# Folds, row maxima and biases of two score tiles at once in the sums pass of a fake-quantised attention

## The chip, the cores and the metric

The kernel runs on one core of a Trainium2 chip. Time is device time in microseconds (us) of one execution of the whole program; lower is better. Engines are named as in the profile: PE (TensorE), DVE (VectorE), ACT (ScalarE), POOL (GpSimd) and SP (SyncE, which issues transfers).

## The reference

The program is a small vision tower: an embedding of 8 images to 8 x 256 tokens of width 192, a first attention with 12 heads whose tensors are all quantised to 8 bits, a mixture of 8 experts, a second attention and a second mixture. Only the first attention is touched. Cut to what matters:

```python
def fake_quant(x):                       # one scale for the whole tensor
    scale = max(|x|) / 127
    return clip(round(x / scale), -127, 127) * scale
scores = einsum('bhqd,bhkd->bhqk', q, k) / sqrt(16)
scores = fake_quant(scores)              # 8 images x 12 heads x 256 x 256
attn = fake_quant(softmax(scores, -1))   # needs the largest weight of all rows
ctx = einsum('bhqk,bhkd->bhqd', attn, v)
```

The quantisation of `attn` needs the greatest softmax weight of the whole tensor before the first weight can be rounded. So the kernel goes over all scores once for the sums of the exponentials (the sums pass), then once more for the weights.

## The kernel before, in words

The program is written engine by engine; each engine runs its own instruction list in order, and semaphores (`wait_ge`, `then_inc`) tie them together. The first attention consists of blocks that follow one another:

- A block takes the greatest score of all 24 tiles (L1022) and, from it, the columns `f_s` and `ns_s`, which hold the scale of the scores.
- The **sums pass** (the block of L1048 to L1145) goes over the same 24 tiles. A tile `n` is four heads of one image: 128 partitions by 8 rows of 256 scores, 2048 values to a partition. PE computes its scores into one half of `pp`, which has two (L922, for the first three images L912); it may overwrite a half when the tile two before has been read. DVE quantises the tile (L1098, from `pp` into `v16t`, which the profile calls `m_pieces`), takes the maximum of its left and right halves into `fold` (L1106), folds 128 to 64 in place (L1114), takes each row's maximum (L1102, `vmax`) and multiplies it to a bias (L1110, `nb`, in the profile `a_nb`). ACT then takes the exponential of each of the eight rows with that bias and adds it up (L1084, eight instructions to a tile, each with an accumulator read).
- DVE's list is interleaved by hand: the steps of tile `n` stand between those of tile `n - 1`, so that a step never follows directly on the one whose result it needs. `v16t`, `vmax` and `nb` have room for all 24 tiles, so DVE never waits for ACT there.
- Behind the tiles, a serial end: reciprocals of the sums of tiles 0 to 22 (L1126) once ACT has finished tile 22, those of the last tile (L1129), a maximum (L1130), an all-reduce on POOL (L1073), a logarithm on ACT (L1089), a split into three parts on DVE (L1137 to L1141), transposes on PE (L1057) and copies (L1144). Then the block of the weights begins (L1183 and on).

ACT's wait before tile `n` is `act.wait_ge(biased, n + 1)`, where `biased` counts the instructions of L1110. The short letters used further down: Q is the quantise step, F the first fold, f the second fold, R the row maxima, B the bias, each with its tile's number.

Of the kernel before, what the change touches and what calls it, by code (L numbers as in the profile page):

```python
# [9 lines left out]
F16 = mybir.dt.float16  # L10
# [3 lines left out]
ALU = mybir.AluOpType  # L14
ACT = mybir.ActivationFunctionType
AX = mybir.AxisListType
# [3 lines left out]
S, D = 256, 192  # L20
T = B * S
P = 128
# [13 lines left out]
HALF = 1536.0  # L36
# [790 lines left out]
def attention0(c, a, scratch, out, proj, pieces, held):  # L827
# [5 lines left out]
    sc, top, peak, room, wout, col = proj.sc, proj.top, proj.peak, proj.room, proj.wout, proj.col  # L833
    with ExitStack() as s:
# [21 lines left out]
        with ExitStack() as s1:  # L856
# [38 lines left out]
            with ExitStack() as s2:  # L895
                TILES = B * H // 4
                mxs = c.sb("a0_mxs", [P, TILES], F32, s2)
                ex = c.sb("a0_ex", [P, 2, 8, S], BF16, s2)
                fold = c.sb("a0_fold", [P, 2, 8, P], F16, s2)
                pp = c.ps("a0_pp", [P, 2, 4, 2 * S], F32, s2)  # L900

                def score(pe, n, k, padded=None):
# [16 lines left out]
                    for j in range(4):  # L919
                        h = 4 * g + j  # L920
                        for qt in range(2):
# [5 lines left out]
                scored, read, chain, peaked, reduced, xrounded, lifted, padded, rounded, stored = (  # L927
                    c.sem(f"a0m_{n}") for n in ("scored", "read", "chain", "peaked", "reduced", "xrounded", "lifted",
                                                "padded", "rounded", "stored"))
                scored_again = c.sem("a0s_scored")  # L930
# [110 lines left out]
                v16t = v16.rearrange("p b (g k) t q -> p (b g) (k t) q", k=4)  # L1041
                vmaxt = vmax[:].rearrange("p b (g k) t -> p (b g) (k t)", k=4)
                nbt = nb[:].rearrange("p b (g k) t -> p (b g) (k t)", k=4)
                sumst = sums[:].rearrange("p b (g k) t -> p (b g) (k t)", k=4)
                c.retire()
                with nc.Block(no_gpsimd_drain=True) as block:

                    @block.tensor  # L1048
                    def _(pe):
                        for n in range(2, TILES):  # L1050
                            pe.wait_ge(read, n - 1)
                            score(pe, n, B + n // 3).then_inc(scored_again, 1)
                        for n in range(2):
                            pe.wait_ge(split, n + 1)
                            for k in range(8):
                                t = 8 * n + k
                                last = nc.tensor.transpose(  # L1057
                                    pr[n][:, k, :], parts[:, t // 2, t % 2].rearrange("p r h -> p (r h)"),
                                    c.identb[:])
                            last.then_inc(turned, 1)  # L1060

                    @block.sync
                    def _(sp):
                        sp.dma_start(sel, a["sel6"]).then_inc(loaded, 16)
                        for img in range(PADDED + 2, B):
                            sp.wait_ge(scored_again, 3 * (img - 1))
                            load_heads(sp, LOADED + img - PADDED)
                        sp.wait_ge(loaded, 16)

                    @block.gpsimd  # L1070
                    def _(pool):
                        pool.wait_ge(peaked, 1)
                        pool.partition_all_reduce(peak[:, 6:7], top[:, 6:7], P, RMAX).then_inc(reduced, 1)  # L1073

                    @block.scalar
                    def _(act):
                        scale = act.alloc_register("a0_scale")
                        act.reg_load(scale, col["s_s"][0:1, :].bitcast(I32))
                        for n in range(TILES):
                            act.wait_ge(biased, n + 1)  # L1080
                            if n >= 2:
                                act.wait_ge(summed, n - 1)
                            for r in range(8):
                                last = act.activation(ex[:, n % 2, r], v16t[:, n, r, :], ACT.Exp,  # L1084
                                                      bias=nbt[:, n, r:r + 1], scale=scale,
                                                      accum_out=sumst[:, n, r:r + 1])
                            last.then_inc(summed, 1)
                        act.wait_ge(scaled, 1)
                        act.activation(flat_lg, rc[:, 0:COUNT], ACT.Ln, scale=col["i_a"]).then_inc(logged, 1)  # L1089

                    @block.vector
                    def _(dve):
                        v = nc.vector
                        link = Chain(dve, chain).link
                        for n in range(TILES + 1):
                            if n < TILES:
                                dve.wait_ge(scored_again, n + 1)
                                v.tensor_scalar(v16t[:, n], pp[:, n % 2].rearrange("p j (t q) -> p (j t) q", q=S),  # L1098
                                                col["f_s"], HALF, ALU.mult, ALU.add).then_inc(read, 1)
                            if n >= 1:  # L1100
                                dve.wait_ge(folded, 2 * n)
                                v.tensor_reduce(vmaxt[:, n - 1], fold[:, (n - 1) % 2, :, 0:P // 2], AX.X, ALU.max)\  # L1102
                                 .then_inc(maxed, 1)
                            if n < TILES:
                                dve.wait_ge(read, n + 1)
                                v.tensor_tensor(fold[:, n % 2], v16t[:, n, :, 0:P], v16t[:, n, :, P:S], ALU.max)\  # L1106
                                 .then_inc(folded, 1)
                            if n >= 1:
                                dve.wait_ge(maxed, n)
                                v.tensor_scalar(nbt[:, n - 1], vmaxt[:, n - 1], col["ns_s"], None, ALU.mult)\  # L1110
                                 .then_inc(biased, 1)
                            if n < TILES:
                                dve.wait_ge(folded, 2 * n + 1)
                                v.tensor_tensor(fold[:, n % 2, :, 0:P // 2], fold[:, n % 2, :, 0:P // 2],  # L1114
                                                fold[:, n % 2, :, P // 2:P], ALU.max).then_inc(folded, 1)
                        dve.wait_ge(biased, TILES)

                        def part(r, n):
                            return parts[:, 4 * n:4 * n + 4, :, r, :].rearrange("p b t h -> p b h t")

                        v.memset(parts[:, :, :, 0, :], -HALF)
                        v.memset(parts[:, :, :, 5, :], 0.0)
                        for n in range(2):
                            v.tensor_scalar(part(1, n), vmax[:, 4 * n:4 * n + 4], -1.0, HALF, ALU.mult, ALU.add)
                        dve.wait_ge(summed, TILES - 1)
                        link(v.reciprocal(rc[:, 0:COUNT - LAST], flat_sums[:, 0:COUNT - LAST]))  # L1126
                        link(v.tensor_reduce(rc[:, COUNT:COUNT + 1], rc[:, 0:COUNT - LAST], AX.X, ALU.max))
                        dve.wait_ge(summed, TILES)
                        link(v.reciprocal(rc[:, COUNT - LAST:COUNT], flat_sums[:, COUNT - LAST:COUNT]))  # L1129
                        v.tensor_reduce(top[:, 6:7], rc[:, COUNT - LAST:COUNT + 1], AX.X, ALU.max).then_inc(peaked, 1)  # L1130
                        dve.wait_ge(reduced, 1)
                        scale_of(link, v, peak[:, 6:7], col["s_a"])
                        v.reciprocal(col["i_a"], col["s_a"]).then_inc(scaled, 1)
                        dve.wait_ge(logged, 1)
                        for n in range(2):
                            rest = lg[:, 4 * n:4 * n + 4]
                            link(v.tensor_scalar(rest, rest, col["i_s"], None, ALU.mult))  # L1137
                            for r in range(2, 4):
                                link(v.tensor_copy(part(r, n), rest))
                                link(v.tensor_tensor(rest, rest, part(r, n), ALU.subtract))  # L1140
                            v.tensor_copy(part(4, n), rest).then_inc(split, 1)  # L1141
                        for n in range(2):
                            dve.wait_ge(turned, n + 1)
                            v.tensor_copy(rows.rearrange("r b (t q) -> r (b t) q", t=2)[:, 8 * n:8 * n + 8, :],  # L1144
                                          pr[n]).then_inc(kept, 1)  # L1145
# [2252 lines left out]
```

## Time and profile before

| | us |
|---|---|
| time, three runs | 1001.4, 1001.75, 1006.43 (median 1001.75) |
| span of the profiled execution, first to last instruction | 1014.8 |
| PE, DVE, ACT, POOL busy in the span | 743.6, 697.2, 672.0, 345.9 |
| first to last exponential of the sums pass (starts) | 170.9 to 264.8 |
| first to last quantise step of the sums pass (starts) | 163.7 to 253.4 |

The three times were taken without the profiler; of the profiled execution only the span is known, and it is 13.05 us (1.3%) longer than the median. Times inside the trace count from the first instruction. A row of the timeline begins with the start and the duration; a duration on DVE or ACT overlaps with the start of the next instruction, so what an instruction costs its engine is read from one start to the next.

### The profile page before, as it was taken

How to read it: one execution, taken by the hardware profiler on the slowest of the kernel's cores; microseconds unless marked ns; L12 is line 12 of the kernel's file. 1: busy time of each engine (PE TensorE's matmuls, PEld its weight loads, DVE VectorE, ACT ScalarE, POOL GpSimd, SP SyncE). 2: the span in 40 equal slices, each digit the busy share in tenths (PEclk: the TensorE clock that was granted, in tenths of full speed). 3: DMA queues.
4: the chain of work that ended last, by engine and by line, in shares of the span. 5: the costliest groups of instructions: out<-in, count | busy, mean ns of one | idle time of the engine just before them, and what ended most of it. 6: DMA issues, size and time to landing. Idle time of an engine off the chain costs nothing. (4 is left out here: it accounts for less than half of the span.)

```text
span 1014.8 us, 19178 instructions
## 1 busy us (share of the span) xinstructions
PE 743.6 (73%) x7062; PEld 537.8 (53%) x7063; DVE 697.2 (69%) x1403; ACT 672.0 (66%) x1229; POOL 345.9 (34%) x260
## 2 busy tenths in 40 slices
PE   2987373344299547999997488867775898999985
PEld 1464141122277324589996444324444467899974
DVE  4159998999599888745443475986998875444542
ACT  1267956999799657755554369578983661676663
POOL 6620460000000000357776424580001202477763
PEclk9979555555599768999999879555556798999999
DMA  5224485000121318623333456380003942233332
GB/s 168 71 90 130 138 234 169 1 23 1 47 75 69 122 45 289 200 54 59 57 56 47 90 233 254 117 297 35 2 2 105 344 169 71 37 54 58 59 45 32
DMA packets 61883, 105.26 MB, mean 104 GB/s; under 512 B 9678, under 2 KB 43618, under 8 KB 61554
## 3 DMA queue, kind: packets, MB, share of 16 engines
q1 hardware_dynamic: 45426, 87.77, 25.6%
q0 software_dynamic: 16384, 16.53, 10.4%
q8 instruction: 45, 0.74, 0.3%
q14 instruction: 28, 0.23, 0.1%
HBM read 76.39 MB, written 27.87 MB: 103 GB/s over the span
## 5 line engine op out<-in xcount | busy, mean ns | idle before, releaser
L2301 DVE COPY m_xgT<-m_px 128x768 f16<-128x768 f16 (+1 forms) x46 | 22.9, 497 | 123.5 <-PE m_px L2146 123.5
L2268 ACT ACTIVATE m_pu<-m_pu,m_b,m_unit 128x256 f32<-128x256 f32 (+1 forms) x138 | 63.5, 509 | 60.9 <-PE m_pu L2178 58.4
L2309 DVE SCALAR_TENSOR_TENSOR m_hT<-m_pu,m_unit,m_hT 128x512 f16<-128x512 f32 (+1 forms) x138 | 86.4, 663 | 17.4 <-ACT m_hT L2261 17.2
L1084 ACT ACTIVATE a_ex<-m_pieces,a_nb 128x256 bf16<-128x256 f16 x192 | 94.6, 560 | 5.4 <-DVE a_nb L1110 5.4
L922 PE MATMUL a_pp<-a_room 16*128 16x256 bf16 x240 | 56.1, 412 | 39.8 <-DVE m_pieces L1098 31.9
L2272 ACT ACTIVATE m_pu<-m_pu,m_unit 128x512 f32<-128x512 f32 (+1 forms) x69 | 41.1, 597 | 62.7 <-PE m_pu L2178 61.7
L2261 ACT ACTIVATE m_hT<-m_pu,m_unit 128x512 f16<-128x512 f32 (+1 forms) x138 | 81.6, 636 | 0.0
L2112 POOL DMA_INDIRECT m_xg<-xn_d,m_token x70 | 70.0, 1000 | 32.1 <-issue 20.6
L2120 POOL DMA_INDIRECT out_h<-m_yo,m_token x39 | 62.1, 1593 | 40.6 <-DVE m_yo L2319 28.8
L2120 POOL DMA_INDIRECT h_d<-m_yo,m_token x39 | 62.1, 1592 | 37.3 <-DVE m_yo L2319 18.0
L2178 PE MATMUL m_pu<-m_xgT,m_w 128*128 128x256 f16 (+1 forms) x690 | 70.4, 261 | 1.3 <-DVE m_xgT L2301 1.3
L2178 PE MATMUL m_pu<-m_xgT,m_pieces 128*128 128x256 f16 (+1 forms) x690 | 67.9, 256 | 1.7 <-issue 1.0
L922 PEld LDWEIGHTS a_pp<-a_room 16*128 16x128 bf16 x240 | 30.3, 136 | 65.6 <-DVE m_pieces L1098 39.0
L2178 PEld LDWEIGHTS m_pu<-m_xgT,m_w 128*128 x690 | 59.7, 100 | 8.8 <-DVE m_xgT L2301 1.7
L2197 PE MATMUL m_py<-m_pieces,m_hT 128*128 x702 | 61.6, 246 | 2.9 <-issue 1.4
L2197 PE MATMUL m_py<-m_w,m_hT 128*128 x702 | 63.0, 246 | 0.0
L2178 PEld LDWEIGHTS m_pu<-m_xgT,m_pieces 128*128 x690 | 58.5, 98 | 8.0 <-issue 1.8
L2197 PEld LDWEIGHTS m_py<-m_pieces,m_hT 128*128 128x128 f16 x702 | 57.4, 98 | 4.3 <-issue 2.6
L2197 PEld LDWEIGHTS m_py<-m_w,m_hT 128*128 128x128 f16 x702 | 58.5, 98 | 0.0
L1098 DVE TENSOR_SCALAR m_pieces<-a_pp,a_sc 128x2048 f16<-128x2048 f32 x24 | 56.4, 2351 | 1.4 <-PEq L931 1.4
L2545 POOL TENSOR_TENSOR hv_parts<-hv_raw,hv_parts 128x1536 f16<-128x1536 f32 (+1 forms) x16 | 43.8, 2739 | 39.3 <-ACT hv_raw L2540 30.3
L1022 DVE TENSOR_REDUCE a_mxs<-a_pp 128x1 f32<-128x2048 f32 x24 | 53.0, 2284 | 1.9 <-PE a_pp L922 1.3
(488 smaller groups left out, 1914.2 us busy)
## 6 DMA issues: line engine op xcount, KB each, us to landing
m_pieces<-in_m_w SPq DMA_DIRECT2D x11, 768.0 KB, 5.1
a_early_w<-in_m_w SPq DMA_DIRECT2D x10, 768.0 KB
hv_raw<-in_m_w SPq DMA_DIRECT2D x8, 768.0 KB, 6.2
w1h_d<-hv_parts SPq DMA_DIRECT2D x8, 768.0 KB, 4.1
m_w<-w1h_d SPq DMA_DIRECT2D x8, 768.0 KB, 9.0
m_pieces<-in_m_w SPq DMA_DIRECT2D x8, 576.0 KB, 5.3
a_room<-in_m_w SPq DMA_DIRECT2D x8, 576.0 KB, 3.6
hv_raw<-in_m_w SPq DMA_DIRECT2D x8, 576.0 KB, 5.9
```

Source lines behind the costliest of these rows:

```text
L922: last = nc.tensor.matmul(pp[:, n % 2, j, qt * S:(qt + 1) * S], qkb[:, load % 2, h, qt * P:(qt + 1) * P], qkb[:, load % 2, H + h, :], star ...
L1022: v.tensor_reduce(mxs[:, n:n + 1], pp[:, n % 2], AX.XY, ALU.max, apply_absolute_value=True).then_inc(read, 1)
L1084: last = act.activation(ex[:, n % 2, r], v16t[:, n, r, :], ACT.Exp, bias=nbt[:, n, r:r + 1], scale=scale, accum_out=sumst[:, n, r:r + 1])
L1098: v.tensor_scalar(v16t[:, n], pp[:, n % 2].rearrange("p j (t q) -> p (j t) q", q=S), col["f_s"], HALF, ALU.mult, ALU.add).then_inc(read, 1)
L2112: pool.indirect_dma_start(xg[:, m % 2, j, :], None, xn_d, bass.IndirectOffsetOnAxis(ap=token[:, n:n + 1], axis=0)).then_inc(got[m % 2], 16)
L2120: pool.indirect_dma_start(total_d, bass.IndirectOffsetOnAxis(ap=token[:, n:n + 1], axis=0), yo[:, m % 2, j, :], None, compute_op=ALU.add). ...
L2178: last = nc.tensor.matmul(pu[:, u, q // 2, (q % 2) * w:(q % 2 + 1) * w], w1_bytes[:, bass.ds(e * (2 * W) + up_place(wpart, tail, q), 2 * P ...
L2197: last = nc.tensor.matmul(py[:, j * D:(j + 1) * D], hT[:, u, hpart, q * w + j * P:q * w + (j + 1) * P], w2_bytes[:, bass.ds(e * (2 * FC * ...
L2261: act.activation(hT[:, u, 0, n * 2 * w:(n + 1) * 2 * w], pu[:, u, n, 0:2 * w], ACT.Identity, scale=unit[:, 1:2]).then_inc(hhigh, 1)
L2268: act.activation(pu[:, u, n, q * w:(q + 1) * w], pu[:, u, n, q * w:(q + 1) * w], ACT.Relu, bias=b1[:, bass.ds(e * FC + 2 * n + q, 1)], sca ...
L2309: last = v.scalar_tensor_tensor(hT[:, u, 1, third], pu[:, u, n, 0:2 * w], unit[:, 1:2], hT[:, u, 0, third], ALU.mult, ALU.subtract)
L2545: self.c.nc.gpsimd.tensor_tensor(parts[:, 1, :], raw, parts[:, 0, :], ALU.subtract).then_inc(self.lowered, 1)
```

## The change

In the sums pass the tiles are put into 14 groups: tiles 0 and 1 alone, ten pairs (2, 3) to (20, 21), tiles 22 and 23 alone. F, f, R and B are done once for a group, so for a pair with twice the width; Q stays one instruction per tile. The second fold gets a tensor of its own, `fold2`, instead of folding in place. ACT's wait before tile `n` becomes a wait for the bias of its group.

```diff
--- before.py
+++ after.py
@@ -897,6 +897,10 @@
                 mxs = c.sb("a0_mxs", [P, TILES], F32, s2)
                 ex = c.sb("a0_ex", [P, 2, 8, S], BF16, s2)
                 fold = c.sb("a0_fold", [P, 2, 8, P], F16, s2)
+                fold2 = c.sb("a0_fold2", [P, 2, 8, P // 2], F16, s2)
+                GROUPS = [(0, 1), (1, 2)] + [(n, n + 2) for n in range(2, TILES - 2, 2)] + \
+                         [(TILES - 2, TILES - 1), (TILES - 1, TILES)]
+                group_of = [g for g, (n0, n1) in enumerate(GROUPS) for _ in range(n0, n1)]
                 pp = c.ps("a0_pp", [P, 2, 4, 2 * S], F32, s2)
 
                 def score(pe, n, k, padded=None):
@@ -1077,7 +1081,7 @@
                         scale = act.alloc_register("a0_scale")
                         act.reg_load(scale, col["s_s"][0:1, :].bitcast(I32))
                         for n in range(TILES):
-                            act.wait_ge(biased, n + 1)
+                            act.wait_ge(biased, group_of[n] + 1)
                             if n >= 2:
                                 act.wait_ge(summed, n - 1)
                             for r in range(8):
@@ -1092,28 +1096,36 @@
                     def _(dve):
                         v = nc.vector
                         link = Chain(dve, chain).link
-                        for n in range(TILES + 1):
-                            if n < TILES:
-                                dve.wait_ge(scored_again, n + 1)
-                                v.tensor_scalar(v16t[:, n], pp[:, n % 2].rearrange("p j (t q) -> p (j t) q", q=S),
-                                                col["f_s"], HALF, ALU.mult, ALU.add).then_inc(read, 1)
-                            if n >= 1:
-                                dve.wait_ge(folded, 2 * n)
-                                v.tensor_reduce(vmaxt[:, n - 1], fold[:, (n - 1) % 2, :, 0:P // 2], AX.X, ALU.max)\
+                        def quantize(n):
+                            dve.wait_ge(scored_again, n + 1)
+                            v.tensor_scalar(v16t[:, n], pp[:, n % 2].rearrange("p j (t q) -> p (j t) q", q=S),
+                                            col["f_s"], HALF, ALU.mult, ALU.add).then_inc(read, 1)
+
+                        for g in range(len(GROUPS) + 1):
+                            n0, n1 = GROUPS[g] if g < len(GROUPS) else (TILES, TILES)
+                            if g >= 1:
+                                p0, p1 = GROUPS[g - 1]
+                                fold_1, fold_2 = fold[:, 0:p1 - p0], fold2[:, 0:p1 - p0]
+                            if n0 < n1:
+                                quantize(n0)
+                            if g >= 1:
+                                dve.wait_ge(folded, 2 * g - 1)
+                                v.tensor_tensor(fold_2, fold_1[:, :, :, 0:P // 2], fold_1[:, :, :, P // 2:P], ALU.max).then_inc(folded, 1)
+                            if n0 + 1 < n1:
+                                quantize(n0 + 1)
+                            if g >= 1:
+                                dve.wait_ge(folded, 2 * g)
+                                v.tensor_reduce(vmaxt[:, p0:p1], fold_2, AX.X, ALU.max)\
                                  .then_inc(maxed, 1)
-                            if n < TILES:
-                                dve.wait_ge(read, n + 1)
-                                v.tensor_tensor(fold[:, n % 2], v16t[:, n, :, 0:P], v16t[:, n, :, P:S], ALU.max)\
-                                 .then_inc(folded, 1)
-                            if n >= 1:
-                                dve.wait_ge(maxed, n)
-                                v.tensor_scalar(nbt[:, n - 1], vmaxt[:, n - 1], col["ns_s"], None, ALU.mult)\
+                            if n0 < n1:
+                                dve.wait_ge(read, n1)
+                                v.tensor_tensor(fold[:, 0:n1 - n0], v16t[:, n0:n1, :, 0:P],
+                                                v16t[:, n0:n1, :, P:S], ALU.max).then_inc(folded, 1)
+                            if g >= 1:
+                                dve.wait_ge(maxed, g)
+                                v.tensor_scalar(nbt[:, p0:p1], vmaxt[:, p0:p1], col["ns_s"], None, ALU.mult)\
                                  .then_inc(biased, 1)
-                            if n < TILES:
-                                dve.wait_ge(folded, 2 * n + 1)
-                                v.tensor_tensor(fold[:, n % 2, :, 0:P // 2], fold[:, n % 2, :, 0:P // 2],
-                                                fold[:, n % 2, :, P // 2:P], ALU.max).then_inc(folded, 1)
-                        dve.wait_ge(biased, TILES)
+                        dve.wait_ge(biased, len(GROUPS))
 
                         def part(r, n):
                             return parts[:, 4 * n:4 * n + 4, :, r, :].rearrange("p b t h -> p b h t")
```

Both lists of DVE begin with the steps of tile 0 and the quantise step of tile 1 (before: Q0, F0, f0, Q1, R0, F1, B0, f1; changed: Q0, F0, Q1, f0, R0, F1, B0). Then, in the kernel before, from the quantise step of tile 2 on; `m_pieces` is the quantised tile, which Q writes and F reads, and the last word of a row is the size of the output:

```order
L1098 TENSOR_SCALAR m_pieces<-a_pp,a_sc 128x2048
L1102 TENSOR_REDUCE a_vmax<-a_fold 128x8
L1106 TENSOR_TENSOR a_fold<-m_pieces 128x1024
L1110 TENSOR_SCALAR a_nb<-a_vmax,a_sc 128x8
L1114 TENSOR_TENSOR a_fold<-a_fold 128x8x64
L1098 TENSOR_SCALAR m_pieces<-a_pp,a_sc 128x2048
L1102 TENSOR_REDUCE a_vmax<-a_fold 128x8
L1106 TENSOR_TENSOR a_fold<-m_pieces 128x1024
L1110 TENSOR_SCALAR a_nb<-a_vmax,a_sc 128x8
L1114 TENSOR_TENSOR a_fold<-a_fold 128x8x64
```

The same stretch of DVE's list in the changed kernel, from the quantise step of tile 2 to the bias of the pair 2, 3:

```order
L1101 TENSOR_SCALAR m_pieces<-a_pp,a_sc 128x2048
L1113 TENSOR_TENSOR a_fold<-a_fold 128x512
L1101 TENSOR_SCALAR m_pieces<-a_pp,a_sc 128x2048
L1118 TENSOR_REDUCE a_vmax<-a_fold 128x8
L1122 TENSOR_TENSOR a_fold<-m_pieces 128x2048
L1126 TENSOR_SCALAR a_nb<-a_vmax,a_sc 128x8
L1101 TENSOR_SCALAR m_pieces<-a_pp,a_sc 128x2048
L1113 TENSOR_TENSOR a_fold<-a_fold 128x1024
L1101 TENSOR_SCALAR m_pieces<-a_pp,a_sc 128x2048
L1118 TENSOR_REDUCE a_vmax<-a_fold 128x16
L1122 TENSOR_TENSOR a_fold<-m_pieces 128x2048
L1126 TENSOR_SCALAR a_nb<-a_vmax,a_sc 128x16
```

Before, the bias of tile 1 (the first L1110 shown) stands behind the quantise step of tile 2 alone. Now it (the first L1126) stands behind those of tiles 2 and 3 and behind the fold of the pair 2, 3, which has 2048 outputs. The bias of tile 2 (before the second L1110 shown, now the L1126 with 128x16) stands behind the quantise steps of tiles up to 3 before and up to 5 now.

The last steps of DVE's list in the changed kernel, from the last pair on:

```order
L1101 TENSOR_SCALAR m_pieces<-a_pp,a_sc 128x2048
L1113 TENSOR_TENSOR a_fold<-a_fold 128x1024
L1118 TENSOR_REDUCE a_vmax<-a_fold 128x16
L1122 TENSOR_TENSOR a_fold<-m_pieces 128x1024
L1126 TENSOR_SCALAR a_nb<-a_vmax,a_sc 128x16
L1101 TENSOR_SCALAR m_pieces<-a_pp,a_sc 128x2048
L1113 TENSOR_TENSOR a_fold<-a_fold 128x512
L1118 TENSOR_REDUCE a_vmax<-a_fold 128x8
L1122 TENSOR_TENSOR a_fold<-m_pieces 128x1024
L1126 TENSOR_SCALAR a_nb<-a_vmax,a_sc 128x8
L1113 TENSOR_TENSOR a_fold<-a_fold 128x512
L1118 TENSOR_REDUCE a_vmax<-a_fold 128x8
```

The bias of the pair 20, 21 (the first row with 128x16 of L1126 here) stands behind one quantise step of tile 22; tiles 22 and 23 follow singly.

## Rows read from the trace of the kernel before

**Rows 1.** Busy time and granted clock, 90 us of the sums pass.

```profile
core 0: us, PE busy (x) PEld busy (x) DVE busy (x) ACT busy (x) POOL busy (x), PEclk, DMA share, GB/s
171.00:261.00 90.00, 31.30 (x160) 15.68 (x160) 88.12 (x117) 90.00 (x367) 0.00 (x0) 0.50 0.03 7
```

**Rows 2.** Instructions by line and shape: busy, mean ns, idle before, releaser.

```profile
L1084 ACT ACTIVATE a_ex<-m_pieces,a_nb 128x256 bf16<-128x256 f16 x192 | 94.6, 560 | 5.4 <-DVE a_nb L1110 5.4
L1098 DVE TENSOR_SCALAR m_pieces<-a_pp,a_sc 128x2048 f16<-128x2048 f32 x24 | 56.4, 2351 | 1.4 <-PEq L931 1.4
L1106 DVE TENSOR_TENSOR a_fold<-m_pieces 128x1024 f16<-128x1024 f16 x24 | 16.5, 689 | 0.0
```

**Rows 3.** Timeline of ACT, start of the sums pass: start, duration.

```profile
170.86 0.51 ACT L1084 ACTIVATE a_ex<-m_pieces,a_nb 128x256 bf16<-128x256 f16 x1 [5.43 <-DVE a_nb L1110]
...
174.32 0.50 ACT L1084 ACTIVATE a_ex<-m_pieces,a_nb 128x256 bf16<-128x256 f16 x1
174.82 0.50 ACT L1084 ACTIVATE a_ex<-m_pieces,a_nb 128x256 bf16<-128x256 f16 x1
```

**Rows 4.** Timeline of DVE, start of the sums pass.

```profile
163.70 2.35 DVE L1098 TENSOR_SCALAR m_pieces<-a_pp,a_sc 128x2048 f16<-128x2048 f32 x1 [1.38 <-PEq L931]
166.08 0.69 DVE L1106 TENSOR_TENSOR a_fold<-m_pieces 128x1024 f16<-128x1024 f16 x1
166.81 0.43 DVE L1114 TENSOR_TENSOR a_fold<-a_fold 128x512 f16<-128x512 f16 x1
167.15 2.34 DVE L1098 TENSOR_SCALAR m_pieces<-a_pp,a_sc 128x2048 f16<-128x2048 f32 x1
169.41 0.68 DVE L1102 TENSOR_REDUCE a_vmax<-a_fold 128x8 f32<-128x512 f16 x1
170.00 0.68 DVE L1106 TENSOR_TENSOR a_fold<-m_pieces 128x1024 f16<-128x1024 f16 x1
170.60 0.22 DVE L1110 TENSOR_SCALAR a_nb<-a_vmax,a_sc 128x8 f32<-128x8 f32 x1
170.74 0.42 DVE L1114 TENSOR_TENSOR a_fold<-a_fold 128x512 f16<-128x512 f16 x1
171.07 2.35 DVE L1098 TENSOR_SCALAR m_pieces<-a_pp,a_sc 128x2048 f16<-128x2048 f32 x1
...
174.52 0.23 DVE L1110 TENSOR_SCALAR a_nb<-a_vmax,a_sc 128x8 f32<-128x8 f32 x1
```

**Rows 5.** Timeline of PE, the scores of a late tile.

```profile
208.77 1.88 PE L922 MATMUL a_pp<-a_room 16*128 16x256 bf16 x8 [2.04 <-DVE m_pieces L1098]
```

**Rows 6.** Timeline of DVE, last tiles and what follows.

```profile
256.87 0.23 DVE L1110 TENSOR_SCALAR a_nb<-a_vmax,a_sc 128x8 f32<-128x8 f32 x1
257.01 0.43 DVE L1114 TENSOR_TENSOR a_fold<-a_fold 128x512 f16<-128x512 f16 x1
257.47 0.69 DVE L1102 TENSOR_REDUCE a_vmax<-a_fold 128x8 f32<-128x512 f16 x1
258.19 0.23 DVE L1110 TENSOR_SCALAR a_nb<-a_vmax,a_sc 128x8 f32<-128x8 f32 x1
...
261.63 1.30 DVE L1126 RECIPROCAL a_early_w<-a_sums 128x184 f32<-128x184 f32 x1 [2.33 <-ACT a_ex L1084]
```

**Rows 7.** Timeline, the end of ACT and the hand-over.

```profile
264.82 0.63 ACT L1084 ACTIVATE a_ex<-m_pieces,a_nb 128x256 bf16<-128x256 f16 x1
265.22 0.32 ACT L1084 ACTIVATION_READ_ACCUMULATOR a_ex<-m_pieces,a_nb 128x1 f32 x1
...
265.65 0.20 DVE L1129 RECIPROCAL a_early_w<-a_sums 128x8 f32<-128x8 f32 x1 [2.33 <-ACT a_ex L1084]
...
273.62 0.58 PE L1183 MATMUL a_pt<-a_early_w 72*128 72x512 bf16 x1 [1.13 <-PEq L1046]
```

**Rows 8.** Shapes near the widened instructions, by line.

```profile
L3053 DVE TENSOR_REDUCE a_neg<-a_pa 128x4 f32<-128x1024 f32 x24 | 29.2, 1219 | 0.0
...
L1943 DVE TENSOR_TENSOR m_tvals<-m_tvals,m_gate 128x624 f16<-128x624 f16 x8 | 6.1, 805 | 0.0
```

## The prediction

> **What bounds the kernel now.** I read the busy time of the engines over the sums pass first, because the change touches nothing else. In 90 us of it ACT is busy for all 90.00 us and DVE for 88.12; PE is busy for a third, and the granted clock is 0.50, the lower of its two levels (1.2 GHz) [rows 1]. So two engines look full, and a table of busy time can't tell which of them sets the end. The list by line tells more: the 192 exponentials of L1084 have 5.4 us of idle time before them in all, in a single wait, for the first bias; DVE's steps L1098 and L1106 have 1.4 and 0.0 [rows 2]. After its first instruction ACT never waits.
>
> The two paces come from starts in the timeline. ACT: the first exponential starts at 170.86, the first of tile 1 at 174.82 [rows 3], the 192nd at 264.82 [rows 7]; 93.96 us over 191 steps is 0.492 us each, 3.935 us a tile. DVE: the bias of tile 0 starts at 170.60 and that of tile 1 at 174.52 [rows 4], 3.92 us a tile. They differ by 0.4%, and ACT is the slower. The bias of tile 1 is ready at 174.52 + 0.23 = 174.75, and ACT takes it at 174.82: DVE delivers just in time at the start, and from there gets ahead by 0.01 us a tile. The last bias is ready at 258.42, the last tile but one starts on ACT about at 257.4, so all of the last tile's 3.9 us run while DVE has no tile work. What ends the pass is ACT: DVE's reciprocals start at 261.63 and 265.65, right behind tiles 22 and 23 [rows 6, 7], and the next block's first matmul at 273.62 follows in series. In the whole stretch the core moves 7 GB/s [rows 1], so no transfer hides a delay. A microsecond more or less at the end of ACT's exponentials is one in the kernel's time.
>
> **The change, part by part.** What DVE's steps cost is read from start to start in [rows 4]: Q 2.26 (167.15 to 169.41), R 0.595 (169.41 to 170.00), F 0.60 (170.00 to 170.60), f 0.335 (170.74 to 171.07), B 0.14 (170.60 to 170.74), the last because f then waits for F. Sum 3.92.
>
> *Removed:* 40 of the 96 narrow steps (14 each of F, f, R, B in place of 24). *Widened:* ten of each. No row shows an f16 maximum of 2048 outputs. From 512 to 1024 outputs a fold goes from 0.335 to 0.60, so 0.52 ns an output and about 0.065 fixed; the fold of a pair is then 0.065 + 2048 x 0.52 = 1.13, its second fold 0.60. R of 1024 inputs: a reduction of that size elsewhere takes 1.219 us where the one of 512 here takes 0.68 [rows 4, 8], 0.54 more, so 1.13. Bounds: simply twice the narrow step (1.20, 0.67, 1.19) on one side, and no fixed part at all, 1.06, 0.53, 1.06, on the other. B I take as 0.10, between 0.07 (half of what it costs now, since f no longer follows at its heels) and 0.14. A pair costs DVE 2 x 2.26 + 0.60 + 1.13 + 1.13 + 0.10 = 7.48 us, against 7.84 before: 0.36 us less. ACT needs 7.87 for it, so in the steady state this saving is worth nothing.
>
> *Moved:* the price is at the start, where there is no lead. Tile 0 hardly changes: f0 goes behind Q1, the dependent pair F0, f0 (0.73 apart, 166.08 to 166.81) is split, so Q1 starts at 166.68, f0 at 168.94, R0 0.46 later (the distance of 257.01 to 257.47 [rows 6]) at 169.40, and B0 at 170.59 as before. ACT starts at 170.86.
>
> Then B1 stands behind Q2, f1, Q3, R1 and the fold of the pair: 170.59 + 0.10 + 2.26 + 0.335 + 2.26 + 0.595 + 1.13 = 177.27. From a bias to ACT it is 0.26 (170.60 to 170.86), so tile 1 starts at 177.53 in place of 174.82: **a stall of 2.71 us**.
>
> B(2,3) stands behind Q4, f(2,3), Q5, R(2,3) and the fold of 4, 5: 177.27 + 0.10 + 2.26 + 0.60 + 2.26 + 1.13 + 1.13 = 184.75. Tile 2 starts at 185.01; ACT ended tile 1 at 177.53 + 3.935 = 181.46: **a second stall of 3.55 us**.
>
> B(4,5) comes 7.48 later, ready for ACT at 192.49; ACT ends tile 3 at 185.01 + 7.87 = 192.88. No third stall, by 0.39 us, and each further pair adds 0.39 to the lead. From here ACT runs 22 tiles through: it ends at 185.01 + 22 x 3.935 = 271.6, before 170.86 + 94.4 = 265.3. The sum is 2.71 + 3.55 = **6.3 us later**. With the bounds of B and of the wide steps: all at the low ends 6.3 - 0.07 x 3 (two wide folds and R) - 0.07 (f) - 0.03 x 2, about 6.0; all at the high ends 6.3 + 0.27 + 0.08 = 6.6, and a pair then costs 7.72, still under 7.87.
>
> What else could wait: PE writes a tile's scores in 1.88 us [rows 5], at the earliest after Q of the tile two before. Between the end of Q2 and the start of Q4 DVE spends f, Q3, R, F and B, about 5.2 us, so PE stays hidden; the loads of further heads, issued by the number of scored tiles, have as many tiles' time as before. At the end DVE delivers B22 and B23 alone and finishes earlier than now, but ACT then lags by more. Instructions of PE, SP, POOL and ACT are the same in number and order.
>
> *A rule and the rows.* DVE's fixed part of 0.065 us a step is what the change saves, 0.36 us a pair. The Trainium skill, "VectorE: DVE Perf Modes", section "The TRN2 errata — SBUF-src ops pay a fixed extra latency per instruction", says that latency is exposed between instructions and that tiles of at least 512 elements spread it out; that speaks for the change. By the rule alone the pass would end earlier with DVE, by about 3.4 us (below); by the rows, which put the end on ACT, it ends 6.3 later. This case's trace agrees that there is such a fixed part.
>
> **The rivals.**
>
> *A. Two stalls, as worked out: +6.3 us.*
>
> *B. DVE sets the pace in a run without the profiler (not slower, or less so).* The profiled span is 1.3% longer than the median, and ACT's lead over DVE as the limit is only 0.4%. Let a tile cost ACT t. Before, the end is the latest of 170.86 + 24t, 257.13 + 2t and 258.45 + t (biases of tiles 22 and 23 [rows 6]). After, B(18,19) is ready at 184.75 + 8 x 7.48 + 0.26 = 244.85, B(20,21) 0.10 + 2.26 + 0.60 + 1.13 + 0.60 and some waiting later, about at 249.7, B23 two narrow groups on, at 255.0; the end is the latest of 185.01 + 22t, 244.85 + 6t, 249.7 + 4t and 255.0 + t. At t = 3.86 the difference is +5.1, at 3.6 +2.1, and it turns at t = 3.07, from 257.13 + 2t = 244.85 + 6t; at 2.5 it is -2.3, and -3.4 is the most that it could ever give. So even a coarser grain of DVE's deliveries takes back what its shorter list gains, unless ACT is a fifth faster than the rows say. Against: the exponentials are 0.49 us apart while DVE works and still when it has stopped (264.82 less 170.86 above spans both), and there is no sign that recording slows them. For: I can't see the pace outside the profile, and 2% less on ACT already brings the loss to 5 us. The point from which it decides is a tile of 3.07 us.
>
> By the same page of the Trainium skill, "VectorE: DVE Perf Modes", same section, an exponential of 256 elements costs ScalarE 224 + 256 cycles at 1.2 GHz, an estimate of 0.40 us; this trace has 0.40 from its start to the start of the accumulator read (264.82 to 265.22 [rows 7]) and 0.09 more for the read. Were the read free outside the profile, the page's figure would make t 3.2 and the change +0.5 us; no run here shows that.
>
> *C. Wide steps cost more than in proportion.* If the f16 maximum lost its rate on this shape, at the price of the nearest slower row, 0.805 us for 624 outputs [rows 8], some 1.04 ns an output, a pair's F would be 2.2 and f 1.13, a pair 9.08 us, above ACT's 7.87. ACT would wait at each pair: B(18,19) at 178.3 + 9 x 9.1 = 260.2, then 5.2 to B(20,21) and four tiles on ACT: 281.4, +16 us. The decision point is 1.54 us for F. Against: the strides of the rows are those of the narrow step, only the count doubles.
>
> *D. The delay is partly given back later.* The block behind starts in series and its engines then wait for each other as before; nothing is in flight that the 6 us could hide. But 750 us of program follow, with clocks that vary, so a few microseconds either way are possible: +2 to +5.
>
> *E. The later program falls better into place and the whole gets over 5 us faster.* No row speaks for it.
>
> **How the numbers follow.** A 0.70, B 0.10, C 0.04, D 0.12, E 0.04. The sum was made against the profiled span: 1014.8 + 6.3 = 1021.1. I carry the same 6.3 to the median of the timed runs, since it consists of waits for DVE steps of fixed length: 1001.75 + 6.3 = 1008.05, **1008.0 us**, 0.63% slower. Half a per cent, 5.0 us, is about what a measurement of this kernel can tell from no change. A's own range is +5 to +7.5; with B and D in it the range goes from 1003.5 to 1010.5, which holds A but for a few hundredths, and most of B and D. Slower by over 0.5%: A but for 0.06 below 5 us, and C: 0.68. Within 0.5%: that 0.06, B and D: 0.28. Faster: E, 0.04.
>
> **What would show it.** In the profile of the changed kernel: ACT's exponentials with two more waits for the bias, 2.7 us before tile 1 and 3.5 us before tile 2, and none after; the folds with 2048 outputs at 1.2 us each by duration; DVE's last bias near 254.7 in place of 258.19, more idle time on DVE before the first reciprocal; the first matmul of the next block at 279.9. A third wait of ACT would mean that a pair costs DVE over 7.87. The prediction is wrong if ACT's pace between the stalls isn't 3.935, or if the time differs from the profile's difference by more than a microsecond or two.

## The result

The changed kernel takes 1008.2 us (median of six runs), the kernel before 1000.8 us in the six runs beside it. The ratio is 1.0069, with a 95% interval of 1.0044 to 1.0094: 4.4 to 9.4 us slower.

The page of the changed kernel begins so:

```profile
span 1007.0 us, 19138 instructions
...
PE 732.1 (73%) x7062; PEld 533.6 (53%) x7063; DVE 695.0 (69%) x1363; ACT 671.4 (67%) x1229; POOL 346.0 (34%) x260
```

Read alone, this misleads: the profiled execution of the slower kernel is 7.8 us shorter than the one shown of before. A span holds the whole program, and what happened outside the pass differed between these two executions by more than the change is worth (the last experiment comes back to it). So everything below is read inside the pass, from the start of the first quantise step to the first matmul of the block behind (L1183 before, L1195 now). I call this the pass length. Before it is 273.62 - 163.70 = 109.9 us [rows 4, 7].

The section on the time before says that the times were taken without the profiler. For its three times no span is on record, but the record gives a span for every timed run of the changed kernel and of the experiments, and in each it is 1.7 to 1.9 us below the time, so spans and times can be compared; the profiled execution of the changed kernel is itself one of the six timed runs (1008.83 us). By the same distance the 1014.8 us shown of before would be a time of about 1016.6 us, an estimate. No timed run of that kernel on record is so long; the longest has 1009.1.

The list by line and shape, in the stretch of the pass (busy, mean ns of one, idle time before it and what ended it):

```profile
L1088 ACT ACTIVATE a_ex<-m_pieces,a_nb 128x256 bf16<-128x256 f16 x192 | 94.4, 492 | 11.6 <-DVE a_nb L1126 11.6
...
L1122 DVE TENSOR_TENSOR a_fold<-m_pieces 128x2048 f16<-128x2048 f16 x10 | 12.1, 1214 | 0.0
L1118 DVE TENSOR_REDUCE a_vmax<-a_fold 128x16 f32<-128x1024 f16 x10 | 12.1, 1208 | 0.0
...
L1113 DVE TENSOR_TENSOR a_fold<-a_fold 128x1024 f16<-128x1024 f16 x10 | 6.8, 679 | 0.0
```

ACT waits 11.6 us for biases instead of 5.4 [rows 2]. The wide steps take 1.21 us by duration, the second fold 0.68.

The timeline of DVE (start, duration):

```profile
154.28 2.35 DVE L1101 TENSOR_SCALAR m_pieces<-a_pp,a_sc 128x2048 f16<-128x2048 f32 x1 [1.89 <-PEq L935]
...
161.19 0.22 DVE L1126 TENSOR_SCALAR a_nb<-a_vmax,a_sc 128x8 f32<-128x8 f32 x1
161.32 2.34 DVE L1101 TENSOR_SCALAR m_pieces<-a_pp,a_sc 128x2048 f16<-128x2048 f32 x1
163.58 0.41 DVE L1113 TENSOR_TENSOR a_fold<-a_fold 128x512 f16<-128x512 f16 x1
163.91 2.34 DVE L1101 TENSOR_SCALAR m_pieces<-a_pp,a_sc 128x2048 f16<-128x2048 f32 x1
166.17 0.68 DVE L1118 TENSOR_REDUCE a_vmax<-a_fold 128x8 f32<-128x512 f16 x1
166.76 1.21 DVE L1122 TENSOR_TENSOR a_fold<-m_pieces 128x2048 f16<-128x2048 f16 x1
167.90 0.22 DVE L1126 TENSOR_SCALAR a_nb<-a_vmax,a_sc 128x8 f32<-128x8 f32 x1
168.03 2.34 DVE L1101 TENSOR_SCALAR m_pieces<-a_pp,a_sc 128x2048 f16<-128x2048 f32 x1
170.29 0.68 DVE L1113 TENSOR_TENSOR a_fold<-a_fold 128x1024 f16<-128x1024 f16 x1
170.89 2.34 DVE L1101 TENSOR_SCALAR m_pieces<-a_pp,a_sc 128x2048 f16<-128x2048 f32 x1
173.15 1.21 DVE L1118 TENSOR_REDUCE a_vmax<-a_fold 128x16 f32<-128x1024 f16 x1
174.28 1.21 DVE L1122 TENSOR_TENSOR a_fold<-m_pieces 128x2048 f16<-128x2048 f16 x1
175.41 0.23 DVE L1126 TENSOR_SCALAR a_nb<-a_vmax,a_sc 128x16 f32<-128x16 f32 x1
...
182.93 0.23 DVE L1126 TENSOR_SCALAR a_nb<-a_vmax,a_sc 128x16 f32<-128x16 f32 x1
...
245.75 0.23 DVE L1126 TENSOR_SCALAR a_nb<-a_vmax,a_sc 128x8 f32<-128x8 f32 x1
...
258.35 1.30 DVE L1138 RECIPROCAL a_early_w<-a_sums 128x184 f32<-128x184 f32 x1 [11.49 <-ACT a_ex L1088]
```

The timeline of ACT, with the three waits that ACT has in the pass, each before the first exponential of a tile (0, 1 and 2), and the last exponential:

```profile
161.44 0.51 ACT L1088 ACTIVATE a_ex<-m_pieces,a_nb 128x256 bf16<-128x256 f16 x1 [5.43 <-DVE a_nb L1126]
...
168.15 0.51 ACT L1088 ACTIVATE a_ex<-m_pieces,a_nb 128x256 bf16<-128x256 f16 x1 [2.67 <-DVE a_nb L1126]
...
175.67 0.51 ACT L1088 ACTIVATE a_ex<-m_pieces,a_nb 128x256 bf16<-128x256 f16 x1 [3.48 <-DVE a_nb L1126]
...
261.67 0.49 ACT L1088 ACTIVATE a_ex<-m_pieces,a_nb 128x256 bf16<-128x256 f16 x1
```

And of PE, the end of the pass:

```profile
270.34 0.58 PE L1195 MATMUL a_pt<-a_early_w 72*128 72x512 bf16 x1 [1.12 <-PEq L1050]
```

The pass length is 270.34 - 154.28 = 116.06 us, 6.1 us more. The two new waits are 2.67 and 3.48 us by these rows. Read from starts they are about 0.1 us longer each: tile 1 starts 13.87 us after the first quantise step (168.15 less 154.28) in place of 11.12 (174.82 less 163.70 [rows 3, 4]), 2.75 later, and tile 2 starts 7.52 after tile 1 (175.67 less 168.15) where a tile's work is 3.93, 3.59 later; 6.3 together. The first experiment shows why the rows name less. From tile 2 on, ACT never waits again, while DVE delivers further and further ahead: its last bias starts 91.5 us after its first quantise step, 3.0 us earlier than the 94.5 of before (258.19 less 163.70 [rows 4, 6]), and then DVE stands idle until its reciprocals at 258.35. DVE became quicker and the kernel slower.

### The profile page after: what moved, and what is told of

Read it like the earlier page. It is cut to its first block and busy times, and to the rows that moved or that the text cites. A ratio compares the mean times of both kernels' runs of the same rounds, so it can differ in the third digit from the quotient of the medians.

```text
span 1007.0 us, 19138 instructions
## 1 busy us (share of the span) xinstructions
PE 732.1 (73%) x7062; PEld 533.6 (53%) x7063; DVE 695.0 (69%) x1363; ACT 671.4 (67%) x1229; POOL 346.0 (34%) x260
## 5 line engine op out<-in xcount | busy, mean ns | idle before, releaser
L1088 ACT ACTIVATE a_ex<-m_pieces,a_nb 128x256 bf16<-128x256 f16 x192 | 94.4, 492 | 11.6 <-DVE a_nb L1126 11.6
```

## The experiments

In all of them the measure is the pass length in the profile, since a stretch between fixed points of one execution can show half a microsecond, where the times of this kernel scatter by several. The times are given beside it; the single pair and the second profile of before have only one timed run each. In the diffs, lines that stay are shortened.

**Every tile alone, in the changed order.** What does the new order of DVE's list cost without any pair?

```diff
-                GROUPS = [(0, 1), (1, 2)] + [(n, n + 2) for n in range(2, TILES - 2, 2)] + \
-                         [(TILES - 2, TILES - 1), (TILES - 1, TILES)]
+                GROUPS = [(n, n + 1) for n in range(TILES)]
```

> The changed kernel with 24 groups of one tile: no wide step, but the changed order of DVE's list, in which the second fold stands between the quantise step and the row maxima that need it. Measure: from the start of the first quantise step to the first matmul of the weights block, 109.9 us before, 116.1 changed. My theory (ACT carries the pass and is hurt by late biases only): no stall at the start, but a tile costs DVE 2.26 + 0.46 + 0.60 + 0.60 + 0.14 = 4.05 us, over ACT's 3.935, so ACT waits 0.12 us before nearly every tile, about 2.5 us in all: 112.4, and the time +2.5 us. Rival (the wide steps or the pairing are not at fault, the new order is): the whole loss stands here already, about 116. Rival (the new order costs nothing): 109.9.

Pass length 265.73 - 153.53 = 112.2 us, close to the 112.4 of my theory; the time is 1.0037 times that of before (0.9997 to 1.0077), so not clear of no change by itself. A tile of DVE's timeline in this run:

```profile
168.53 0.23 DVE L1125 TENSOR_SCALAR a_nb<-a_vmax,a_sc 128x8 f32<-128x8 f32 x1
168.66 2.35 DVE L1100 TENSOR_SCALAR m_pieces<-a_pp,a_sc 128x2048 f16<-128x2048 f32 x1
170.92 0.41 DVE L1112 TENSOR_TENSOR a_fold<-a_fold 128x512 f16<-128x512 f16 x1
171.37 0.69 DVE L1117 TENSOR_REDUCE a_vmax<-a_fold 128x8 f32<-128x512 f16 x1
171.97 0.68 DVE L1121 TENSOR_TENSOR a_fold<-m_pieces 128x1024 f16<-128x1024 f16 x1
172.57 0.22 DVE L1125 TENSOR_SCALAR a_nb<-a_vmax,a_sc 128x8 f32<-128x8 f32 x1
```

From one bias to the next it is 4.04 us. The second fold to the row maxima takes 0.45 instead of 0.33, because the latter needs the former's result. ACT (at the change from tile 0 to 1, and from 1 to 2):

```profile
164.15 0.49 ACT L1087 ACTIVATE a_ex<-m_pieces,a_nb 128x256 bf16<-128x256 f16 x1
...
164.74 0.51 ACT L1087 ACTIVATE a_ex<-m_pieces,a_nb 128x256 bf16<-128x256 f16 x1
...
168.20 0.49 ACT L1087 ACTIVATE a_ex<-m_pieces,a_nb 128x256 bf16<-128x256 f16 x1
...
168.79 0.51 ACT L1087 ACTIVATE a_ex<-m_pieces,a_nb 128x256 bf16<-128x256 f16 x1
```

The steps over a tile's border are 0.59 us instead of 0.49. No row names this as a wait, since an instruction's recorded duration covers it: starts must be read, not idle times. So the order costs 2.3 us when no group is wide. In the changed kernel it costs nothing, since there a second quantise step stands between the two in the turn of every pair.

**Pairs from tile 12 on, the order of before ahead of them.** Is the loss paid per pair, at the start of the pass, or once?

```diff
+                GROUPS = [(n, n + 1) for n in range(12)] + [(n, n + 2) for n in range(12, TILES - 2, 2)] + \
+                         [(TILES - 2, TILES - 1), (TILES - 1, TILES)]
...
-                            if g >= 1:
+                            if g >= 1 and p1 - p0 == 2:
                                 dve.wait_ge(folded, 2 * g - 1)
                                 v.tensor_tensor(fold_2, fold_1[...], fold_1[...], ALU.max).then_inc(folded, 1)
...
+                            if n1 - n0 == 1:
+                                dve.wait_ge(folded, 2 * g + 1)
+                                v.tensor_tensor(fold2[:, 0:1], fold[...], fold[...], ALU.max).then_inc(folded, 1)
```

> Tiles 0 to 11 alone in the order of before, pairs from (12, 13) to (20, 21), 22 and 23 alone: five pairs in place of ten. My theory (the loss is an entry fee, paid once wherever pairs begin, since ACT's lead over DVE as the limit never grows): no wait of ACT before tile 12 but its first, a stall of 2.6 us before tile 11 and of 3.5 us before tile 12, no other; the measure 116.0, the time +6 us. Rival (each wide group costs something, so the loss goes with the number of pairs): about half, 113. Rival (the loss comes of the start of the pass, with PE and DVE still filling up, and later pairs are free): 109.9.

All waits of ACT in this run:

```profile
159.74 0.51 ACT L1088 ACTIVATE a_ex<-m_pieces,a_nb 128x256 bf16<-128x256 f16 x1 [5.43 <-DVE a_nb L1126]
...
205.67 0.51 ACT L1088 ACTIVATE a_ex<-m_pieces,a_nb 128x256 bf16<-128x256 f16 x1 [2.59 <-DVE a_nb L1126]
...
213.18 0.51 ACT L1088 ACTIVATE a_ex<-m_pieces,a_nb 128x256 bf16<-128x256 f16 x1 [3.47 <-DVE a_nb L1126]
```

None for tiles 1 to 10, then 2.59 us before tile 11 and 3.47 before tile 12, none behind. Pass length 268.52 - 152.57 = 115.95 us, the time 1.0087 times that of before (1.0049 to 1.0125). With half the pairs, and with the first of them in the middle of a running pass, the loss is the same 6 us. It is neither a price per pair nor one of the pass's start.

**A single pair, 12 and 13.** The same kernel with `[(12, 14)]` between single tiles.

> Only tiles 12 and 13 as a pair, all others alone in the order of before. My theory: a stall of 2.6 us before tile 11; then the bias of the pair stands behind one quantise step only, 0.14 + 2.26 + 0.73 + 1.13 + 0.60 = 4.86 us after that of tile 11, against 3.935 of ACT's work: a stall of 0.9 us. Together 3.5, the measure 113.4. Rival (a fee for each pair, 0.63 us): 110.5.

ACT before tiles 11 and 12:

```profile
209.46 0.51 ACT L1087 ACTIVATE a_ex<-m_pieces,a_nb 128x256 bf16<-128x256 f16 x1 [2.59 <-DVE a_nb L1125]
...
214.30 0.51 ACT L1087 ACTIVATE a_ex<-m_pieces,a_nb 128x256 bf16<-128x256 f16 x1 [0.81 <-DVE a_nb L1125]
```

2.59 and 0.81 us, pass length 269.65 - 156.36 = 113.3 (the one timed run has 1003.4 us, too little to compare). One pair out of ten costs 3.4 of the 6.1 us, over half of the whole loss. The second wait is shorter than with pairs behind it, because only one quantise step and one narrow fold stand ahead of the pair's bias.

**The bias of the group before, ahead of the second quantise step.** Can the two waits be parted?

```diff
                             if g >= 1:
                                 v.tensor_reduce(vmaxt[:, p0:p1], fold_2, AX.X, ALU.max).then_inc(maxed, 1)
+                                dve.wait_ge(maxed, g)
+                                v.tensor_scalar(nbt[:, p0:p1], vmaxt[:, p0:p1], ...).then_inc(biased, 1)
+                            if n0 + 1 < n1:
+                                quantize(n0 + 1)
                             if n0 < n1:
                                 v.tensor_tensor(fold[:, 0:n1 - n0], ...).then_inc(folded, 1)
-                            if g >= 1:
-                                dve.wait_ge(maxed, g)
-                                v.tensor_scalar(nbt[:, p0:p1], vmaxt[:, p0:p1], ...).then_inc(biased, 1)
```

> The changed kernel, but in a pair's turn the row maxima and the bias of the group before come ahead of the second quantise step. My theory: B1 comes 3.5 us after B0, so the first stall (2.7 us) is gone; the bias of the pair 2, 3 still needs two quantise steps and a wide fold: about 7.85 us after B1, a stall of 3.5 us before tile 2 remains, and a pair costs DVE 7.86 us, just ACT's pace, so nothing is made good later. The measure 113.4, the time +3.5 us. Rival (the two stalls are one delay that only moves): ACT waits 6.3 us before tile 2, the measure 116.1.

ACT's waits (all that the trace names):

```profile
162.09 0.51 ACT L1088 ACTIVATE a_ex<-m_pieces,a_nb 128x256 bf16<-128x256 f16 x1 [4.96 <-DVE a_nb L1119]
...
174.15 0.51 ACT L1088 ACTIVATE a_ex<-m_pieces,a_nb 128x256 bf16<-128x256 f16 x1 [3.85 <-DVE a_nb L1119]
```

And the first exponential of tile 1, for which it names none:

```profile
166.26 0.51 ACT L1088 ACTIVATE a_ex<-m_pieces,a_nb 128x256 bf16<-128x256 f16 x1
```

The wait before tile 1 is all but gone and the one before tile 2 is 3.85 us, not 6.3. By starts, tile 1 still comes 4.17 us after tile 0 (162.09 to 166.26) instead of 3.96 [rows 3]: B1 starts 4.17 us after B0, not 3.5, because the fold of tile 1, 0.60 us, also stands between them; 3.5 is what the other steps add up to. ACT also starts 0.5 us earlier (6.69 us after the first quantise step, 7.16 before [rows 3, 4]), as B0 no longer stands behind a fold. Pass length 269.12 - 155.40 = 113.7 us, 0.3 more than I gave it, but the parts were off by more and made up for each other. Against the second profile of before, by starts, ACT begins 0.5 us earlier, loses 0.2 at tile 1 and 4.0 at tile 2 (3.5 in the sum), and about 0.3 over the rest: a pair costs DVE 7.90 us here (biases at 173.88 and 181.78), 0.03 over ACT's 7.87, so DVE carries the rest of the pass in small steps. Time 1.0045 times before (1.0010 to 1.0081). Better than the changed kernel by its pass, still slower than before.

**Half of ACT's work, with single tiles and with pairs.** Does the shorter list of DVE gain anything where DVE carries the pass? Four of eight exponentials are left out in both kernels, and the sums of those rows are a constant, so what the two compute is not the reference.

```diff
                         v.memset(half[:], HALF)
+                        v.memset(sums[:], 100.0)
...
-                            for r in range(8):
+                            for r in range(4):
                                 last = act.activation(ex[:, n % 2, r], v16t[:, n, r, :], ACT.Exp, ...)
```

> The kernel before, with exponentials for four of the eight rows of each tile only (the sums of the other rows are a constant, 100): ACT's tile costs 1.97 us, half. DVE's list of the pass is as it was. Base for the next run. My theory: DVE now carries the pass at 3.92 us a tile, ACT waits before every tile, about 45 us in all; the end comes 1.97 us after the last bias is ready. The measure (first quantise step to first matmul of the weights block) 105.4 against 109.9.

> The changed kernel with the same exponentials left out. My theory: where DVE carries the pass, its shorter list counts: the last bias comes 3.4 us earlier after the first quantise step, so the measure is 3.4 us below that of the run with single tiles, 102.0, and the time lower by 3 to 4 us. That is the rival of the prediction in which DVE sets the pace. Against it: if pairs cost by their late biases whatever ACT's load, this run is the slower of the two, by up to 6 us.

Single tiles, two neighbouring waits of ACT:

```profile
173.30 0.51 ACT L1085 ACTIVATE a_ex<-m_pieces,a_nb 128x256 bf16<-128x256 f16 x1 [1.84 <-DVE a_nb L1111]
...
177.22 0.51 ACT L1085 ACTIVATE a_ex<-m_pieces,a_nb 128x256 bf16<-128x256 f16 x1 [1.85 <-DVE a_nb L1111]
```

With pairs:

```profile
181.86 0.51 ACT L1089 ACTIVATE a_ex<-m_pieces,a_nb 128x256 bf16<-128x256 f16 x1 [3.48 <-DVE a_nb L1127]
...
189.38 0.51 ACT L1089 ACTIVATE a_ex<-m_pieces,a_nb 128x256 bf16<-128x256 f16 x1 [3.48 <-DVE a_nb L1127]
```

By its rows ACT waits 1.85 us for each tile, or 3.48 us for each pair, 46.1 and 44.1 us in all, the wait for the first bias included. Biases now arrive every 3.92 us for one tile and every 7.52 us for two. Pass lengths 259.94 - 154.37 = 105.6 and 255.49 - 152.95 = 102.5 us: the same change that costs 6.1 us behind a full ACT gains 3.0 behind a half-full one. The times say so too: medians 998.3 and 994.9 us, ratios to the kernel before 0.9989 (0.9958 to 1.0021) and 0.9947 (0.9929 to 0.9965). The two are equal outside the pass and are best compared with each other, not with the kernel before: halving ACT's work alone makes the pass 4.1 to 4.3 us shorter (105.6 for 109.7 and 109.9), but the time only 0.9 us by the medians, with an interval that reaches 4.2; whether anything was lost outside the pass, and where, is open. I had 3.4 for the gain; B costs 0.14 us a pair and not 0.10.

**The kernel before, profiled again.**

> The kernel before, unchanged, profiled once more. The profile shown of it spans 1014.8 us, the changed kernel's 1007.0, though the latter is slower by its times. My theory: that first profiled execution was slow outside the pass, which starts at 163.7 us in it against 152.6 to 156.4 in six other profiles; this one should start the pass near 154, take 109.9 us for it and span about 1001. Rival (the kernel before is really slower outside the pass, and the change gives that back): the pass starts near 163 again and the span is near 1014. ACT's durations, which grew from 0.51 to 0.63 us through the pass in the first profile with starts 0.49 apart: 0.49 throughout if that was the execution's own, growing again if it belongs to a pass that ACT works through without a wait.

The two ends of the pass in this profile, and the row of the exponentials:

```profile
154.26 2.35 DVE L1098 TENSOR_SCALAR m_pieces<-a_pp,a_sc 128x2048 f16<-128x2048 f32 x1 [1.41 <-PEq L931]
...
263.93 0.58 PE L1183 MATMUL a_pt<-a_early_w 72*128 72x512 bf16 x1 [1.12 <-PEq L1046]
...
L1084 ACT ACTIVATE a_ex<-m_pieces,a_nb 128x256 bf16<-128x256 f16 x192 | 94.3, 493 | 5.4 <-DVE a_nb L1110 5.4
```

The pass starts at 154.26 us, is 263.93 - 154.26 = 109.7 us long, and the span is 997.1 us (time 998.9). So the profile shown of before was slow outside the pass, by 9.4 us ahead of it and by 8.0 us behind it (1014.8 - 273.62 = 741.2 against 997.1 - 263.93 = 733.2). Inside the pass the two agree within 0.25 us. Against this second profile the pass of the changed kernel is 6.4 us longer, with the first it is 6.1.

## Why the prediction was right

- **ACT carries the pass, not DVE.** Shown from both sides: 3.0 us less on DVE's list bought nothing with ACT's work whole, and all of it with ACT's work halved.
- **The first stall, 2.71 us.** Measured 2.75 by starts, as the sum counts it (2.67 by the row). B1 came 13.62 us after the first quantise step (13.57 in the sum).
- **The second stall, 3.55 us.** Measured 3.59 by starts (3.48 by the row), with B(2,3) 21.13 us after the first quantise step (21.05).
- **No third stall.** None. The later pairs are free, but only because the entry was paid: this is what the run with pairs from tile 12 adds. The prediction had it as arithmetic.
- **The wide steps.** 1.13, 1.13 and 0.60 us from start to start, as extrapolated, since the rate per element held for twice the size. B was mis-sized: 0.13 to 0.14, the upper end of its bounds, not 0.10; the reason given for the lower price, that the next step no longer depends on the one before it, is not borne out. A pair costs DVE 7.52 us, not 7.48, and the last bias came at 91.5 us in place of 91.0. Behind ACT this only made the two stalls about 0.04 us longer each.
- **PE stays hidden.** So it does: from the end of Q2 to the start of Q4 there are 4.45 us (163.58 to 168.03), not 5.2, which is the figure of a later pair. No quantise step behind it waits for scores, as the even 7.52 us a pair show.
- **The sum, 6.3 us.** 6.1 against the first profile, 6.4 against the second; the timed ratio gives 6.9 (4.4 to 9.4). That 1008.0 met the measured 1008.2 so closely is in part luck: the difference of the medians is 7.4 us, 1.1 more than forecast, and the median of before, 1001.75 in three runs, came out 0.9 lower in six.
- **Rival B (DVE sets the pace without the profiler).** The times exclude its forecast of a gain. Its ground falls away as well: the profiled execution of the changed kernel is one of its timed runs, 0.6 us above their median, so the pace of ACT in the trace is that of a timed run. The mechanism is real, and halving ACT's work brought it out. The claim that its formula can give -3.4 us at most is wrong: worked through, it gives -3.5 at ACT's halved tile of 1.97 us and -3.9 at 1.77. The measured gain was 3.0, since each of ten pairs costs 0.04 us more than in the formula.
- **Rivals C, D and E.** C is excluded by the rows of the wide steps. The times exclude E, a gain of over 5 us. Of D, a loss of 2 to 5 us, they leave only the upper end, from 4.4; the profiles can't decide there, since the length behind the pass, 1007.0 - 270.34 = 736.7 us, lies between those of the two profiles of before (733.2 and 741.2), which are further apart than what D gives back.
- **The span.** One step failed: I carried 6.3 us to the profiled span and wrote 1021.1. It was 1007.0. The span of before on which that stood was 17.7 us above that of another execution of the same kernel, and all but 0.25 of the excess lay outside the pass. The moments 254.7 and 279.9, forecast for the last bias and for the next block's first matmul, came at 245.75 and 270.34, over 9 us early, because the pass itself began 9.4 us earlier. I had seen that the span was 1.3% above the median and took it for something that both profiles would share.

No version was found that beats the kernel before. Each single tile or pair that is handed over must be ready within ACT's 3.935 us a tile, and before the change DVE meets that with 0.04 us to spare at tile 1 (174.52 + 0.26 = 174.78, against 174.82 [rows 3, 4]; the prediction's 0.07 takes the end of the bias's record and not the 0.26 us that ACT starts behind it). Taking the bias forward starts ACT 0.5 us earlier, but I see no order of the same steps in which the biases of tiles 1 and 2 also come earlier. Moving folds to POOL, which is idle in the pass, was not tried.

## What to carry to other kernels

Where a producer feeds a consumer at almost the same pace, making the producer's steps coarser saves its fixed costs but delays its first results, and the delay is paid in full if the consumer is the one without slack. Look for who waits for whom before widening: the gain appears only on an engine that somebody waits for, and the price only where the consumer has no backlog. It isn't paid again for each group, so widening later doesn't help and widening fewer helps little: here five pairs cost as much as ten, and a single one over half of that. And compare the stretch that was changed between two fixed points of each trace, not spans: here the span had the wrong sign. Read such waits from starts too: a tenth of a microsecond of each was hidden in the record of the instruction before it.

## What was not expected of the hardware

In the first profile of before, the exponentials' recorded durations grew from 0.51 us to 0.63 through the pass (mean 0.560 [rows 2, 3, 7]), while their starts stayed 0.49 apart. In the second profile of the same kernel they are 0.493 in the mean, with the same starts, and in the changed kernel 0.49. So the growth belonged to that execution. It cost next to nothing: the pass is 0.25 us longer than in the second profile, and 0.14 of that stands behind the last exponential, whose record is 0.14 longer (0.63 against 0.49). Its cause is open. It is one more reason to read an engine's pace from starts.

A bias of 8 or 16 values costs DVE 0.13 to 0.14 us from its start to that of an independent quantise step (161.19 to 161.32, 167.90 to 168.03), about the same as the 0.14 up to the dependent fold before the change [rows 4].
